# GpSimd instead of VectorE multiplies the turned tokens by 1/std

## The reference, cut to what matters

```python
xn = _layernorm(x, axis=-1)                    # (x - m) / sqrt(v + eps), no learned scale
x = x + attention(xn, w_attn, w_proj, decay_raw) + experts(xn, W1, W2, Wr)

# attention, for each batch b and head h (16 heads of width 8)
q, k, v = split(xn @ w_attn)
scores = q @ k.T / sqrt(8) + causal - log1p(softplus(decay_raw) * log1p(distance))
y = softmax(scores) @ v ; attention = y @ w_proj

# experts: the two best of 8 by softmax(xn @ Wr.T), weights normalised to sum 1
h = silu(xn @ W1[e].T) ; y = h @ W2[e].T
```

## Time and profile before

| | |
|---|---|
| median of 3 runs | 508.23 us (507.23 to 508.44) |
| the profiled execution: its own time | 508.83 us |
| its span in the profile | 507.1 us |
| TensorE busy | 480.4 us, 95% of the span |
| VectorE busy | 366.5 us, 72% |
| GpSimd busy | 364.6 us, 72% |
| ScalarE busy | 336.6 us, 66% |
| the chain that ended last | PE 71%, DVE 16%, ACT 9%, issue 3% |

### The profile page before, as it was taken

The page is one execution under the profiler, slowest core; times in us unless marked ns, Lnnn a source line. Parts: engine busy times, 40 slices in busy tenths (PEclk is TensorE's granted clock), DMA queues, the critical chain, the costliest instruction groups (busy, mean ns, idle before and its releaser), DMA issues.

```text
span 507.1 us, 13438 instructions
## 1 busy us (share of the span) xinstructions
PE 480.4 (95%) x4300; PEld 348.5 (69%) x4300; DVE 366.5 (72%) x1406; ACT 336.6 (66%) x620; POOL 364.6 (72%) x592
## 2 busy tenths in 40 slices
PE   6859899899999999999999999989999999999997
PEld 5735565565665566466656656689999999999554
DVE  6897989988999989989888897833333333333887
ACT  5948878788888888888888888753232333332772
POOL 2388788789888888888889888734555554545784
PEclk9987999999999999999999999999999999999999
DMA  6497590681471452354154063877666677672635
GB/s 187 137 338 198 164 255 9 181 220 37 137 203 34 143 162 81 101 161 118 71 169 144 30 197 112 223 223 235 195 208 211 208 209 212 185 215 73 235 123 144
DMA packets 72755, 82.24 MB, mean 162 GB/s; under 512 B 8638, under 2 KB 52704, under 8 KB 72688
## 3 DMA queue, kind: packets, MB, share of 16 engines
q1 hardware_dynamic: 68368, 72.91, 49.6%
q0 software_dynamic: 4320, 8.47, 4.7%
HBM read 49.94 MB, written 31.86 MB: 161 GB/s over the span
## 4 chain that ended last, share of the span: by engine, by line
PE 71%; DVE 16%; ACT 9%; issue 3%; POOL 0%; ACTq 0%; DVEq 0%; POOLq 0%
PE psT L1491 22%; PE psT L1580 13%; PE ps L1553 12%; PE psO L1513 11%; DVE scores L1261 8%; PE ps L1463 6%; ACT probs L1002 4%; ACT scores L957 2%; PE psM L1439 2%; DVE x_all L604 2%; PE ps L1544 1%; DVE xt L1118 1%; ACT values L984 1%; PE ps L1367 1%; PE ps L1410 1%
## 5 line engine op out<-in xcount | busy, mean ns | idle before, releaser
L1261 DVE CUSTOM_DVE_ANT_0 scores<-ps,wdist 128x256 f32<-128x256 f32 (+3 forms) x512 | 217.2, 485 | 23.4 <-PE ps L1463 22.8
L1002 ACT ACTIVATE probs<-psT 128x512 f32<-128x512 f32 x320 | 173.9, 596 | 51.0 <-PE psT L1491 49.9
L872 POOL TENSOR_SCALAR scores<-scores,row_max 128x256 f32<-128x256 f32 (+3 forms) x388 | 183.9, 488 | 32.3 <-DVE row_max L1261 31.2
L1491 PE MATMUL psT<-ident,scores 128*128 128x128 f32 x1280 | 178.2, 283 | 7.0 <-ACT probs L1002 5.8
L1491 PEld LDWEIGHTS psT<-ident,scores 128*128 128x128 f32 x1280 | 139.2, 142 | 64.8 <-issue 44.9
L891 POOL DMA_INDIRECT picked_dram<-scores,row_ring x71 | 69.8, 983 | 70.7 <-DVE scores L1342 67.5
L1011 ACT ACTIVATE scores<-ps 128x512 f32<-128x512 f32 x71 | 42.3, 597 | 92.1 <-PE ps L1553 92.1
L1513 PE MATMUL psO<-probs,values 128*32 128x512 f32 (+3 forms) x1024 | 88.4, 441 | 0.0
L957 ACT ACTIVATE scores<-scores,row_max 128x512 f32<-128x512 f32 x124 | 82.9, 726 | 0.0
L1580 PE MATMUL psT<-xn_all,scores 128*128 x568 | 75.5, 276 | 2.1 <-ACT scores L1011 1.9
L1553 PE MATMUL ps<-scores,wdist 128*128 128x128 f32 x568 | 74.9, 275 | 0.3 <-DVE scores L1330 0.3
(11 more groups left out here) (164 smaller groups left out, 296.8 us busy)
## 6 DMA issues: line engine op xcount, KB each, us to landing
wdist<-w1t SPq DMA_DIRECT2D x71, 256.0 KB, 3.5
k_rows<-k_dram SPq DMA_DIRECT2D x64, 96.0 KB, 2.9
q_rows<-q_dram SPq DMA_DIRECT2D x64, 96.0 KB, 2.6
row_ring<-rows_dram SPq DMA_DIRECT2D x71, 65.0 KB, 3.1
rows_dram<-row_ring SPq DMA_DIRECT2D x6, 650.0 KB, 5.9
k_dram<-k_parts SPq DMA_DIRECT2D x7, 384.0 KB, 2.4
q_dram<-q_parts SPq DMA_DIRECT2D x7, 384.0 KB, 2.6
xn_all<-picked_dram SPq DMA_DIRECT2D x4, 512.0 KB, 7.6
```

The costliest lines, as they stand in the source:

```text
L872: last = nc.gpsimd.tensor_scalar(part, part, -1.0, row_max[:, r, tile, quad:quad + 1], ALU.mult, ALU.add)
L1002: nc.scalar.activation(probs[:, at.ring(2), w, :], psT[:, w % 2], ACT.Exp, scale=-1.0).then_inc(exp_ready, 1)
L1261: last = nc.vector.tensor_tensor_reduce(out=scores[:, r, u, col:col + n], in0=bank[:, col:col + n], in1=wdist[:, at.g * QUADS + quad, SEQ ...
L1491: last = nc.tensor.transpose(psT[:, w % 2, place * P:(place + 1) * P], scores[:, at.ring(2), u, col + key * P:col + (key + 1) * P], ident[:])
```

## The change

`scale_tokens` goes from VectorE to GpSimd, with the same waits and the same operands, and in `slot_steps` its row goes from behind `p1(4)` to ahead of it. In slot 0 it stood behind `p1(3)` already and stays there.

```diff
@@ slot_steps @@
     step("PV", n - 2, NGROUP, 2)
+    per_batch("XN", -4)
     p1(4)
-    per_batch("XN", -4)
     step("TE", n - 1, NGROUP, 6, 8)
@@ GpSimd @@
+                def scale_tokens(at):
+
+                    b = at.c // GROUPS
+                    pool.wait_ge(scales_loaded, 16 * b)
+                    if b == 1:
+                        pool.wait_ge(xt_copied, 2)
+                        pool.wait_ge(vl_full, 2)
+                    else:
+                        pool.wait_ge(xt_loaded, 16 * (b - 1))
+                    nc.gpsimd.tensor_tensor(xt[:, at.parity, :], xt[:, at.parity, :], yt[:], ALU.mult).then_inc(xt_scaled, 1)
...
-                run_slots({"RS": rstd_step, "CZ": causal_step, "LC": logits_step, "P1": less_step, "NR": rows_step, "SC": send_step,
+                run_slots({"RS": rstd_step, "CZ": causal_step, "LC": logits_step, "XN": scale_tokens, "P1": less_step, "NR": rows_step, "SC": send_step,
@@ VectorE @@
-                def scale_tokens(at):
...
-                    v.tensor_tensor(xt[:, at.parity, :], xt[:, at.parity, :], yt[:], ALU.mult).then_inc(xt_scaled, 1)
...
-                                "QR": rest_step("QA", 2, q_parts), "QL": lo_step("QA", 2, q_parts), "XN": scale_tokens, "V0": first_values}
+                                "QR": rest_step("QA", 2, q_parts), "QL": lo_step("QA", 2, q_parts), "V0": first_values}
```

## The result

The changed kernel takes 510.22 us, the median of 10 runs (509.37 to 511.74), against 508.29 us for the kernel before beside it (10 runs, 507.23 to 509.58): ratio 1.0039, 95% interval 1.0027 to 1.005. The forecast was 507.8 us, range 505.7 to 509.9. So the change makes the kernel slower, and the time lies outside the range. The same program was measured twice more, beside new runs of the kernel before: 508.85 us, ratio 1.0024 [1.0013, 1.0035], and 509.73 us, ratio 1.0023 [1.0009, 1.0036]. Its loss is thus between 1.1 and 1.9 us. These two times lie inside the range, but they too are slower, where the forecast was faster.

The account below looks back on a forecast made before the run. The prediction took TensorE, busy for 95% of the span, as the bound. Its terms -1.48 + 0.8 + 0.2 = -0.5 us on the profiled 508.83 gave 508.3, and on the median 507.8 us, range 505.7 to 509.9.

Parts of the forecast that it names:

- The multiplication on GpSimd: Each moved multiplication was to take 1.33 us on GpSimd, not below VectorE's own 0.69.
- The bound above: GpSimd's multiplication could exceed 1.33 us by as much as a VectorE instruction blocks it, say 0.3 us.
- Slots 12 and 16: Removing VectorE's long multiplication gains 1.16 us each; GpSimd's lateness gives back 0.42 each; net gain 1.48 us.
- the undisturbed 10.02 us: Time between first turns at the same place of slots 20 and 21, with the same work, against 11.18 from group 12.
- wait for GpSimd's pieces: Sign of being right: group 13's first turns some 10.4 us behind group 12's, with a wait for line 883.
- What is late next: In slot 13, GpSimd's 0.70 us of idle time ahead of unit 8 was to take up the rest of its lateness.
- Slot 4: GpSimd's multiplication blocks VectorE's gates, so `p1(4)` begins 0.85 us later; taken as +0.8 us, bound below 0.
- Slots 0 and 1: At the start, the keys' matmul waits for GpSimd until about 36.7, turn 2 comes at 38.7 against 38.47: +0.2 us.
- the slower rival: Clock of 0.50 granted from 44.93 to 48.34: +1.2 us; from two such stretches +2.9, or 511.1 us; chance 0.13.
- Slots 8, 20 and 24: The move was to be free here: GpSimd's next units come some 0.9 us late, with a margin of 0.85 us.
- Behind the span: Time after the span: the prediction had no term for it and applied -0.5 us to the profiled execution's 508.83 us.

## Why the prediction was wrong, and where it was right

It had the engines, the places and most sizes right, and two terms were missing.

**The multiplication on GpSimd**: predicted 1.33 us, measured 1.27, nearly constant. The bound above, that VectorE would block it, was not touched.

**Slots 12 and 16**: the sum had -1.16 and +0.42 each, -0.74 net. Measured -0.69 and -0.68, with waits of 0.19 us for the multiplication where 0.24 was expected. The mechanism was right. The shares were a little otherwise: against the undisturbed 10.02 us, the keys' matmul is 0.36 late (0.24 expected) and the rest of the way 0.11 (0.18 expected), and TensorE shows no wait for GpSimd's pieces ahead of the first turns of group 13, which was named as a sign.

**What is late next** is the first step that failed. The text said that GpSimd's idle time in slot 13 "takes up the rest of the lateness". It did, but VectorE's `y_q` multiplication (line 1302), which had met the end of a row of four pieces, now met a row of twelve without a gap. The sum had priced that kind of blocking for the gates, and did not ask it of the other VectorE instructions with two SBUF inputs. It measured +0.44 a time, +0.88 in all. The link from line 1302 to TensorE's wait is read from traces: in all nine traces in which GpSimd multiplies batches 4 and 5, line 1302 takes 0.94 to 1.08 us there and 0.35 to 0.44 is lost in the next slot; with the order alone it takes 0.65 and 0.06 is lost, and where it takes 0.48 nothing is. No kernel took it away by itself. By the Trainium skill ("SBUF — State Buffer", section "SBUF: two separate sides") the port pair that the two engines share is held for one whole instruction by whichever started first. The 1.08 us fit that: they are 0.60 longer than 0.48, not much more than one piece of 0.47 us (5.69 / 12). The 2.92 us before don't: they are 2.2 longer than 0.69, several pieces, and there the measurement decides.

**Slot 4**: predicted +0.8 with gates of 1.0 us; measured 0.83 us for the gates, +0.63 in the slot and +0.43 once slot 5 has made up 0.2. With the gates behind `p1(4)` the cost was gone. This step was right in its mechanism, and its size was 0.43 of the 0.8.

**Slots 0 and 1**: predicted +0.2, measured -0.2 at group 1, and that by luck. The keys' matmul came at 36.34, where 36.7 was expected, but its two matmuls took 2.04 us at the lower clock, where 1.50 was taken, and turn 2 came at 39.28, not 38.7. What made up for it, the clock that was back at 41.24 instead of 44.93, the prediction didn't have. The stretch from 44.93 was granted 1.00, so the slower rival did not come about as it was put.

**Slots 8, 20 and 24** were to be free; 0.14 us appear ahead of group 26. Together this gives -0.69 - 0.68 + 0.88 + 0.43 - 0.16 + 0.14 = -0.1 us up to group 28, as the rows say (321.49 - 321.56). The forecast had -0.5.

**Behind the span** is the second step that failed, and the larger one: the difference between own time and span was carried over from the kernel before as if the change could not touch it. It grew by 0.8 us. The change took 14 executed instructions from VectorE (7 multiplications, 7 waits) and gave 14 to GpSimd. VectorE's last load of instructions comes 5.0 us ahead of the end, when it has begun 1,475 of them, in before and in the kernels with memsets. The changed VectorE ends at 1,469, and this load falls into what follows the span; and GpSimd's longer program brings one more. The count alone is not the rule: with batches 4 and 5 on GpSimd the load still stands 5.0 us ahead of the end, with 1,471 of 1,479 begun. The two additions tell them apart: GpSimd's 14 instructions alone bring 0.43 us (2.15 - 1.72), and VectorE's shorter program 0.35 (2.52 - 2.17), 0.8 together. That a load is what is waited for there is the likeliest reading of the table, not its proof: seven instructions on GpSimd bring 0.2 us with no load behind the span, with batches 2 to 7 there are two loads and only 0.2, and the change with late gates has the changed kernel's two loads and 2.34 us, not 2.52.

**What stays open.** Of the loss of 1.1 to 1.9 us, 0.8 are behind the span. The median span itself is longer than that of before by 1.1, 0.2 and 0.9 us in the three measurements of the changed program. The attention accounts for about nothing of this in three of the four traces of the changed program, and for 0.7 in the fourth, where it is there from the first turns on. The experts' stage stood to before at +1.4, -0.6, +0.3 and -0.4 us in the same four. So some half a microsecond inside the span is not explained by these, and scatter of single executions is as large as that.

The likeliest source is the start, and the one execution of before that I compared with hides it. From the first turns of group 0 to those of group 1 the seven traces with batch 1 on GpSimd all take 15.56 to 15.62 us. The nine traces with batch 1 on VectorE fall into two kinds: five, the profiled execution of before among them, take 15.36 to 15.76, with the clock back at 1.00 from 43.6 to 45.2, and four take 14.38 to 14.68, with the clock back from 42.1 to 43.2. The mean of the nine is 15.12, that is 0.48 less. So the multiplication of batch 1 on GpSimd seems to cost about half a microsecond on average by taking the quick starts away. That fits the 0.4 us by which the median span with batches 2 to 7 was shorter, but no kernel tested it alone, and 16 single executions are few.

## What to carry to other kernels

Before moving work onto an engine, list every instruction of its neighbour that can be blocked by it, at the place itself and over the next slot, where the engine is late: removing one stall of this kind moved it to the next instruction of the kind. Ask of each moved step whether all its instances need the move: two of seven gave all of the gain and the other five only cost. Moving the transfers that made GpSimd late gained about as much as moving the multiplication (0.60 against 0.70 us by the traces), and the two added up. Where differences are below 0.3%, compare own time less span too: if it changed, look at the transfers behind the end of the span. And take more than one trace of the kernel before: its start alone comes in two kinds, 1 us apart.

## What the runs showed of the hardware

- The length of an engine's program can cost at the end. 14 small memsets on GpSimd, in slots with room for them, lengthened what lies behind the span from 1.72 to 2.15 us. With 14 instructions more on GpSimd and 14 less on VectorE it was 2.52, and 2.17 once VectorE had 14 memsets in their place.
- VectorE's copy of 128x512 took 2.03 us beside GpSimd's pieces and 0.43 us at 32.74, ahead of them: with the multiplication gone from its way it came before GpSimd's row of pieces.
- VectorE's multiplication of 128x512 took 0.84 us when it began 1.4 us into GpSimd's row of twelve pieces, 2.58 to 2.97 us when it began 2.8 to 3.1 us into it, and 0.77 to 0.82 us when it began 4.0 us into it.
- TensorE's granted clock at the start was 0.50 from 31.27, 1.00 from 34.69, 0.50 from 38.10 and 1.00 from 44.93 in the profiled execution of the kernel before; in eight others with the same steps there it was back for good between 42.1 and 45.2. In the changed kernel, where TensorE idled for 2.62 us ahead of 36.34, it was 0.50 from 31.00 to 41.24 and 1.00 from there. Eight turns took 1.97 us at the one level and 1.09 at the other.
- Nops on VectorE, asked for 22 times, left no instruction in the trace, and neither did GpSimd's 71.
